# Attention masks added by TensorE inside the score banks, another opening, one routed expert moved, and later places in a decoder layer

## The reference

```python
k = _l2norm(silu(x @ Wk)); q = silu(x @ Wq); v = silu(x @ Wv); a = k * gamma
def step(S, inp):                         # scan over the tokens
    bs1 = einsum('bhk,bhkv->bhv', kt, S);  S1 = S + at[..., :, None] * bs1[..., None, :]
    S2 = exp(gft)[..., None] * S1
    bs2 = einsum('bhk,bhkv->bhv', kt, S2); S3 = S2 + at * bs2 + kt * vt
    o = einsum('bhk,bhkv->bhv', qt, S3)
out3 = stack([z, z, o]).reshape(B, 3*N, H, HD); out = out3[:, -N:]   # o of the tokens from 683 on
...
scores = q @ k^T / sqrt(HD); masked entries out; softmax; @ v; @ Wo + bo
...
top-2 of sigmoid(x @ centroids) + bias; gelu(x @ Wfc) @ Wproj of 2 shared and 2 chosen experts
```

## Time and profile before

| | |
|---|---|
| median of the runs | 2340.8 us |
| the profiled execution's own time | 2338.4 us |
| its span, first to last instruction | 2336.6 us |
| DVE busy | 2012.8 us (86%) |
| PE busy | 1754.3 us (75%) |
| POOL busy | 1189.1 us (51%) |
| ACT busy | 683.9 us (29%) |
| mean granted TensorE clock | 0.856 |

### The profile page before, as it was taken

How to read it: one execution, slowest core, us unless ns; L and a number is a source line. 1 busy time by engine, 2 the same in 40 slices (tenths; PEclk the granted TensorE clock), 3 DMA queues, 4 the chain that set the end, 5 groups by cost and what they waited for, 6 DMA issues and landing times.

```text
span 2336.6 us, 33767 instructions
## 1 busy us (share of the span) xinstructions
PE 1754.3 (75%) x10398; PEld 1333.6 (57%) x10398; DVE 2012.8 (86%) x5733; ACT 683.9 (29%) x1363; POOL 1189.1 (51%) x1487
## 2 busy tenths in 40 slices
PE   4258988998789879988998340268887699668993
PEld 2145766676667666766677220145575467555673
DVE  5999999999999999999999998999999989932000
ACT  1132234323432343234323110171223622143120
POOL 2544454565456545654675479473675655222203
PEclk8568999999999999998999765567998689977997
DMA  8100442344234423442345120000254024431353
GB/s 263 42 1 10 140 143 86 107 150 143 84 109 146 143 84 110 148 142 82 108 147 174 44 96 14 21 1 5 102 175 137 1 77 142 135 115 59 108 182 106
DMA packets 175118, 238.65 MB, mean 102 GB/s; under 512 B 28657, under 2 KB 148074, under 8 KB 174954
## 3 DMA queue, kind: packets, MB, share of 16 engines
q1 hardware_dynamic: 140874, 194.46, 24.6%
q10 hardware_dynamic: 27936, 25.44, 3.3%
q0 software_dynamic: 6144, 16.79, 2.2%
HBM read 202.09 MB, written 33.16 MB: 101 GB/s over the span
## 4 chain that ended last, share of the span: by engine, by line
DVE 52%; PE 22%; POOL 10%; issue 7%; ACT 6%; DMA 2%; SPq 0%; POOLq 0%; ACTq 0%; DVEq 0%; PEldq 0%
DVE ps L1610 11%; DVE ps L1591 10%; DVE prod L1583 7%; DVE terms L1598 7%; PE ps L646 4%; DVE terms L1593 4%; PE ps L637 4%; PE ps L582 2%; PE ps L573 2%; DVE rec_out L1537 2%; DVE rec_in L1537 2%; PE ps L519 2%; DVE oprod L1563 2%; ACT eT L847 1%; PE ps L530 1%
## 5 line engine op out<-in xcount | busy, mean ns | idle before, releaser
L1610 DVE TENSOR_REDUCE ps<-terms 128x64 f32<-128x320 f32 x1024 | 449.6, 485 | 0.0
L1591 DVE TENSOR_REDUCE ps<-prod 128x16 f32<-128x272 f32 x1024 | 398.3, 435 | 0.0
L1598 DVE TENSOR_TENSOR terms<-ps,rec_out 128x256 f32<-128x256 f32 x1024 | 382.8, 417 | 0.0
L1583 DVE TENSOR_TENSOR prod<-ps,rec_in 128x256 f32<-128x256 f32 x1024 | 381.9, 416 | 0.0
L637 PE MATMUL ps<-xg,fc 128*128 128x128 f32 x2848 | 351.6, 284 | 27.5 <-PE ps L646 11.9
L637 PEld LDWEIGHTS ps<-xg,fc 128*128 128x128 f32 x2848 | 341.4, 199 | 48.9 <-issue 41.2
L646 PE MATMUL ps<-pj,hT 128*128 128x256 f32 x1424 | 335.0, 389 | 33.2 <-ACT hT L926 33.2
L646 PEld LDWEIGHTS ps<-pj,hT 128*128 128x128 f32 x1424 | 266.3, 192 | 86.4 <-ACT hT L926 52.9
L573 PE MATMUL ps<-xtf,fc 128*128 128x512 f32 x512 | 244.1, 615 | 7.0 <-ACT hT L874 3.7
L582 PE MATMUL ps<-pj,hT 128*128 128x256 f32 x1024 | 238.9, 385 | 0.0
L582 PEld LDWEIGHTS ps<-pj,hT 128*128 128x128 f32 x1024 | 196.4, 193 | 57.5 <-issue 34.4
(11 more groups left out here) (235 smaller groups left out, 3061.0 us busy)
## 6 DMA issues: line engine op xcount, KB each, us to landing
fc<-in_wfcT SPq DMA_DIRECT2D x80, 1024.0 KB, 5.1
pj<-in_wpT SPq DMA_DIRECT2D x80, 1024.0 KB, 7.9
xg_rows<-in_rows ACTq DMA_DIRECT2D x105, 128.0 KB, 2.1
out_rows<-y ACTq DMA_DIRECT2D x89, 128.0 KB, 5.6
in_rows<-o_rows SPq DMA_DIRECT2D x2, 2176.0 KB, 17.4
out_rows<-o_rows SPq DMA_DIRECT2D x2, 2176.0 KB, 17.1
xtp<-in_xT SPq DMA_DIRECT2D x32, 128.0 KB, 2.6
xin<-in_x SPq DMA_DIRECT2D x8, 512.0 KB, 6.6
```

Of the source, the lines that this page charges most:

```text
L1583: tt(prod[:, c % PLACED, :, cols, 0:HD], SE[:, old, cols, 0:HD].unsqueeze(1).to_broadcast([P, NV, HC, HD]), rec_in[:, c].unsqueeze(2).to_b ...
L1591: red(SE[:, old, cols, HD:EH].rearrange("p v n -> p n v"), prod[:, c % PLACED, :, cols, 0:HD + 1], AX.X, ALU.add).then_inc(step_done, 1)
L1598: tt(terms[:, cols, :, 0:NV], SE[:, old, cols, HD:EH].unsqueeze(2).to_broadcast([P, HC, HD, NV]), rec_out[:, c].unsqueeze(1).to_broadcast( ...
L1610: red(SE[:, new, cols, 0:HD], terms[:, cols, :, 0:NV + 1], AX.X, ALU.add).then_inc(step_done, 1)
```

## The change

There are four parts.

1. **Masks.** For tiles 5 to 7 PE writes the mask into the score banks before the scores: for each group two products of the identity with `cap`, 308 columns each, and the query products are added to them. DVE's addition and its wait are gone.
2. **Opening.** The weights for keys and values are loaded second, those for queries later. PE makes keys, then values (`prepare_first`). ACT takes the keys' activation first, and a square root in place of POOL's power; DVE does the whole norm. The context's keys and values are made by ACT (`context`).
3. **Experts.** Tile 6 does experts 2 to 8 in its own period and leaves one, expert 9, which stands behind `start` in the tail; nothing stands behind `finish` there. SP's order follows it: `outputs(1)` of period 7 stands behind the reloads of experts 6 and 7.
4. **Places.** In the tables for bound tiles minima, divided, resid and routing stand later.

```diff
-REST = NE - 2
-BEHIND = {False: EXPERTS[LATE:], True: (REST, None, None, REST + 1, None)}
+FREE_REST = EXPERTS[LATE:]
+REST_OF = {FIRST_BOUND: (NE - 2, None, None, NE - 1, None), FIRST_BOUND + 1: (NE - 1, None, None, None, None), LAST: ()}
+def own_of(tile):
+    return EXPERTS[NSH:NE - len(rest_of(tile))]
...
             def period(p, m=None, f=None, load=None, bound=False, ahead=R, stores=(None,) * R):
...
-                    outputs(1)
-                    for e in EXPERTS[6:REST]:
+                    if f is None:
+                        outputs(1)
+                    for e in EXPERTS[6:8]:
                         used(m, e)
+                    if f is not None:
+                        outputs(1)
+                    if m != LAST:
+                        for e in own_of(m)[6:]:
+                            used(m, e)
...
-            for dst, src in ((w_f1, wf1), (w_g, wg), (w_kv, wkv), (w_q, wqr)):
+            for dst, src in ((w_kv, wkv), (w_f1, wf1), (w_g, wg)):
...
             def scores(m):

+                masked = m >= FIRST_BOUND
+                if masked:
+                    pe.wait_ge(cap_done, m + 1)
...
+                        if masked:
+                            for j in range(2):
+                                mm(ps[:, (UP, A0)[two] + j, 0:2 * QK * SK], ident[:, :], cap[:, b].unsqueeze(1).to_broadcast([P, 2 * QK, SK]),
+                                   start=True, stop=False)
...
-                                       start=True, stop=True, tile_position=(rows.start, 0))
+                                       start=not masked, stop=not masked or half == 1, tile_position=(rows.start, 0))
...
+            def prepare_first():
...
+                act.wait_ge(first_ps, 1)
+                fn(k, ps[:, KV[0], :].rearrange("p (i d) -> p i d", i=CH), ACT.Silu).then_inc(first_k, 1)
+                act.wait_ge(prep_pool, 3)
+                fn(hsum[:, 1], hsum[:, 0], ACT.Sqrt).then_inc(first_root, 1)
+                act.wait_ge(xf1_sb, 2 * CH)
+                fn(beta[:, :, :], graw[:, :, :], ACT.Sigmoid).then_inc(fq_sb, 1)
...
             def minima(t, m, at):
...
                         if m >= FIRST_BOUND:
-                            dve.wait_ge(cap_done, m + 1)
                             dve.wait_ge(sc_sb, m * (2 * B) + (2 * b + 2))
-                            tt(probs[:, b], probs[:, b], cap[:, b].unsqueeze(1).to_broadcast([P, H, SK]), ALU.add).then_inc(capped, 1)
-                        dve.wait_ge(capped, m * B + (b + 1))
+                        else:
+                            dve.wait_ge(capped, m * B + (b + 1))
                         red(least[:, b], probs[:, b], AX.X, ALU.min).then_inc(min_done, 1)
...
             def first_preparation():
...
+                dve.wait_ge(first_k, 1)
+                then(tt(zp[:, :], k, k, ALU.mult))
+                sums(hsum[:, 0])
...
+                then(nc.vector.tensor_scalar(hsum[:, 0], hsum[:, 0], NORM_EPS * NORM_EPS, None, ALU.max))
+                dve.wait_ge(first_root, 1)
+                then(nc.vector.reciprocal(hsum[:, 1], hsum[:, 1]))
...
-BOUND_AT = {"gated": 3, 0: 3, "x_plus": 12, 1: 13, "minima": (22, 22, 23, 24), "divided": 44, "resid": 53, 2: 53, "routing": 60, "places": 64, "rows": 65, "scatter": 66}
-LATER_AT = {"gated": 3, 0: 3, "x_plus": 13, 1: 13, "minima": (21, 22, 23, 24), "divided": 43, "resid": 49, 2: 49, "routing": 55, "places": 63, "rows": 63, "gather": 54, "scatter": 63, "combine": 66, 3: 75}
+BOUND_AT = {"gated": 3, 0: 3, "x_plus": 12, 1: 13, "minima": (22, 23, 24, 25), "divided": 48, "resid": 55, 2: 55, "routing": 62, "places": 64, "rows": 65, "scatter": 66}
+LATER_AT = {"gated": 3, 0: 3, "x_plus": 13, 1: 13, "minima": (22, 24, 25, 27), "divided": 46, "resid": 53, 2: 53, "routing": 60, "places": 63, "rows": 63, "gather": 54, "scatter": 63, "combine": 66, 3: 75}
```

More of the change, by code:

```diff
@@ L79, with rest_of @@
 LATE = NE - 5
-REST = NE - 2
-BEHIND = {False: EXPERTS[LATE:], True: (REST, None, None, REST + 1, None)}
+FREE_REST = EXPERTS[LATE:]
+REST_OF = {FIRST_BOUND: (NE - 2, None, None, NE - 1, None), FIRST_BOUND + 1: (NE - 1, None, None, None, None), LAST: ()}
+def rest_of(tile):
+    return [e for e in REST_OF.get(tile, FREE_REST) if e is not None]
+def own_of(tile):
+    return EXPERTS[NSH:NE - len(rest_of(tile))]
 STEP = 8
@@ L343, in period @@
                 if bound:
-                    used(f, REST)
+                    rest = rest_of(f) if f is not None else []
+                    for e in rest[:-1]:
+                        used(f, e)
                     if load is not None:
                         next_tile(load)
-                    used(f, REST + 1)
+                    for e in rest[-1:]:
+                        used(f, e)
                     outputs(0)
@@ L440, in prepare, with keys_or_values @@
                     mm(ps[:, low[i], D:2 * D], xf1T[:, i], w_f2, start=True, stop=True).then_inc(prep_b_ps, 1)
+            def prepare_first():
+                low = LOW[False]
+                xt = [[xtp[:, c].rearrange("p b (n i) -> p i b n", i=CH)[:, i] for c in range(KC)] for i in range(CH)]
+                def keys_or_values(half):
+                    for i in range(CH):
+                        for c in range(KC):
+                            ins = mm(ps[:, KV[half], i * D:(i + 1) * D], xt[i][c], w_kv[:, c, half * D:(half + 1) * D],
+                                     start=c == 0, stop=c == KC - 1)
+                    ins.then_inc(first_ps, 1)
+                pe.wait_ge(xt_in, 16 * KC)
+                for i in range(CH):
+                    for c in range(KC):
+                        mm(ps[0:HD, low[i], 0:P], w_f1[:, c], xt[i][c], start=c == 0, stop=c == KC - 1)
+                    for c in range(KC):
+                        ins = mm(ps[:, low[i], P:P + H], xt[i][c], w_g[:, c], start=c == 0, stop=c == KC - 1)
+                    ins.then_inc(prep_a_ps, 1)
+                keys_or_values(0)
+                for i in range(CH):
+                    pe.wait_ge(xf1_sb, i * 2 + 2)
+                    mm(ps[:, low[i], D:2 * D], xf1T[:, i], w_f2, start=True, stop=True).then_inc(prep_b_ps, 1)
+                keys_or_values(1)
             def turn(src, done):
@@ L718, in second @@
                         prep(2)
-                last_experts(f, (start, attend, weigh, finish, second), BEHIND[bound])
+                last_experts(f, (start, attend, weigh, finish, second), REST_OF.get(f, FREE_REST))
                 if m is not None:
@@ L736, in period @@
                 if m is not None:
-                    own = EXPERTS[NSH:NE if m == LAST else REST if bound else LATE]
+                    own = own_of(m)
                     bounds_of = bounds_of_tile[m]
@@ L984, in second @@
                         prep(2)
-                hi = last_experts(f, (start, attend, weigh, lambda: None, second), BEHIND[bound])
+                hi = last_experts(f, (start, attend, weigh, lambda: None, second), REST_OF.get(f, FREE_REST))
                 if bound and f is not None:
@@ L1009, in _ @@
             act.sem_inc(y_stored, 1)
-            prepare(0)
+            prepare_first()
+            context()
             act.wait_ge(pool_const, 1)
-            act.wait_ge(xattn_w_in, 10 * 16)
+            act.wait_ge(xattn_w_in, 11 * 16)
             for c in range(KC):
@@ L1246, in _ @@
             pool.wait_ge(pool_set, consts)
-            for i, op in enumerate(preparations(0)[:PREP_NORMS]):
-                prepare(0, i, op)
             def period(p, m=None, f=None, bound=False, keep=False):
@@ L1477, in first_preparation @@
                 k, w, e, z = vec[:, :, K_COL], vec[:, :, W_COL], vec[:, :, E_COL], vec[:, 0, W_COL:K_COL + 1]
-                done = PREP_NORMS
+                done = 0
                 def then(ins):
```

59 lines of the change are left out of this document (37 added, 22 removed).

## The result

The changed kernel takes 2332.5 us (median of 18 runs, 2322.1 to 2338.5), the kernel before beside it 2339.5 (18 runs, 2336.8 to 2344.2). The ratio is 0.9963, 95% interval 0.9951 to 0.9974: **7 us faster, where 27.5 were forecast**.

What follows compares the result with a forecast made beforehand. The chain was taken as opening, DVE's unbroken scan, then tail, with DVE holding 52% of the span. Gains of 13.8 (opening), 9.4 (scan) and 4.3 (tail) make 27.5: 2338.4 - 27.5 = 2310.9, plus 2.4: 2313 us, range 2304 to 2327.

Steps and rivals of the forecast that it cites:

- Opening: Start of the kernel: DVE reaches the first product with the decay at 19.7 instead of 33.54, 13.8 us earlier.
- what follows it is unchanged: Behind the start of the opening's layout: the transposes, then the scan, run as before.
- Router and experts: Tail: with no expert ahead, the router starts with the norm, -8.3 us; expert 8 hides in PE's idleness before the tail.
- The score stage: Tiles 5 to 7: a group takes 1.58 us with masks, 13.6 from first score product to last copy, 7.9 before.
- The 4 us a tile: Bound tiles' scores: by the skill's rule 32 bare weight loads of 0.13 us each, some 10 us higher over three tiles.
- Waits in the scan: DVE in periods 6 and 7: 4.6 of 14.0 us of removed additions turn into waits, leaving 9.4 us gained.
- The gate rows' clock: PE's gate rows behind the scores run at the upper clock: 4.5 us come back in period 6, 2.7 in period 7.
- waits eat the masks' gain: Rival in the scan: lower clock in one tile or bare identity loads, DVE gains nothing, 2322 us; chance 15%.
- Tail: Behind the scan: last score copy 5.7 us later, 1.67 of POOL wait gone, the chain then as before: +4.0 us.
- the lower clock: Rival in all three tiles' score stages: masks at PE's lower clock, 24.4 us a tile instead of 13.6, 2352 us; chance 4%.
- PE doesn't get done before the scan: Rival at the scan's end: expert 7 or 8 ends late, a pass of 8.8 us enters the chain, 2321 us; chance 7%.
- through 4 us before the scan: Scan's end: expert 7, behind which the store of the recurrence's outputs waits, ends 4 us before the scan.

Runs made afterwards that it cites:

- open_only: The kernel before with the new opening alone (prepare_first, context on ACT, new order of loads): 2326.0 us, ratio 0.9943 to before.
- f_none: The changed kernel with masks back on DVE and the old places, so opening and experts alone: 2322.6 us, ratio 0.9920 to before.
- experts_only: The kernel before with the experts' move alone, masks on DVE, opening and places as before: 2338.4 us, ratio 0.9981 to before.
- f_scan: The changed kernel with f32 masks on PE in tiles 5 and 6 only, DVE's additions in tile 7: 2323.5 us, ratio 0.9929 to before.
- tail_masks: The changed kernel with f32 masks on PE in tile 7 alone and the old places: 2334.7 us, ratio 0.9966 to before.
- store_first: The changed kernel with the recurrence's last store queued ahead of the load of expert 9's weights: 2329.7 us, ratio 0.9956 to before.
- rep: The changed kernel once more, unaltered, for a second profile: 2340.7 us, ratio 0.9988 to before.
- bf16_masks: The changed kernel with identity and mask of the mask products in bf16, scores still f32: 2325.2 us, ratio 0.9931 to before.
- masks_places: The kernel before with masks on PE and the new places, opening and experts as before: 2346.7 us, ratio 1.0026 to before.
- the square: Four kernels on one chip, all with opening and experts, f32 masks on PE in scan or not, tail or not: 2322.6, 2323.5, 2334.7, 2333.4 us.
- f_all: The changed kernel once more, f32 masks on PE in tiles 5 to 7: 2333.4 us, ratio 0.9966 to before.
- bf16_scan: The changed kernel with bf16 masks on PE in tiles 5 and 6, DVE's additions in tile 7: 2312.2 us, ratio 0.9883 to before.
- best: bf16_scan with the store of the recurrence's rows ahead of expert 9's weights: 2311.5 us, ratio 0.9874 to before.

## Why the prediction was wrong

**Opening: right.** Forecast 13.8 us, 13.94 in the profile at the layout's start, 13.4 by the ratio of `open_only`, which leaves 8.4 to 18.3 open. Its strings came out item by item: keys at 14.62 (14.6), ACT late with decay and beta (19.27; 19.4), DVE at the decay at 19.52 (19.7). That "what follows it is unchanged" is less sure. From there to the layout that opens period 6, where DVE has the same work, it is 1414 to 1417 us in the four profiles with the old opening (mean 1415.5) and 1415 to 1421 in the fourteen with the new one (mean 1417.8): some 2 us may be given back on the way, but the ranges overlap.

**Router and experts: right by the mechanism.** In the tail, from the residual sum behind the attention to the number of passes, it is 31.2 us before and 23.4 in `f_none`: 7.8, where 8.3 were forecast. Expert 8 is hidden, with 15.8 us of PE's idleness left in `f_none` and 9.05 in the changed kernel, 5 to 8 forecast. With no expert ahead PE stands 6.43 us and turns the rows at the lower level (1.94 instead of 1.06); that was in the forecast, whose 6.7 us to the shared experts came from such a turn and measure 6.65. What it lacked is this: in `experts_only` the stretch from that turn to the passes takes 20.6 us, in `f_none` 17.0, so only 4 of the 8 us are had. PE isn't the reason. Its rows up to the router's last product are the same in both (turn 1.94, router product 1.96, granted clock 0.67). But in `experts_only` ACT reads the router's result 1.9 us after it is made instead of at once, and four of DVE's small routing operations last 1.6 to 2.3 us, where each takes 0.19 in `f_none`. One of them, and what POOL does beside it:

```profile
2149.80 4.82 POOL L1091 TENSOR_TENSOR y_out<-y_out,y_back 128x1024 f32<-128x1024 f32 x2
2149.91 2.27 DVE L1411 TENSOR_TENSOR rbuf<-rbuf,index 128x32 f32<-128x32 f32 x1
```

In all profiles with the new order of experts such stretched operations lie inside POOL's two products of `y_back` and `y_out`, which combine tile 6's outputs. With the router's result read early, DVE starts 2.8 to 3.2 us ahead of the first of these and is through with the choice in time (the first profile of the changed kernel, `f_none`, `f_scan`, `tail_masks`, `store_first`); with it late by 2 us DVE starts 1.0 us ahead and loses the most (`experts_only`, `rep`, `bf16_masks`). So the earlier router has moved up against POOL's work; no run moves POOL's products to prove it, and why ACT reads late in some executions is open.

**The score stage: the step that failed.** The forecast took "A group's scores take 0.41" by halving a row of sixteen instructions, added 1.17 for the masks and got 1.58. The masks were nearly right (1.23). The 0.41 was never the time of one group: it is half of what two take side by side, and with a product of all 128 rows between them each takes its own 0.72. It makes 16.5 us of 13.6, in each of the three tiles. The page "TensorE: Matmul & The Clock Gate" of the Trainium skill, section "Part 3: Packing small matmuls — row/col tiling", says that a weight load overlaps a product in flight only if it goes to other row groups. Behind the mask products the rows agree: the small weights' loads begin with 0.42 us of idleness after the last mask load in f32 and 0.27 in bf16, together with the first small product. Against it stand, as the forecast said, the full-width turns, eight loads and eight product instructions in 1.06 us; but such turns have no two groups side by side to lose, so they couldn't price this. Nor is it shown that the bare loads cost anything here, as a group is 0.79 long with and without a mask product ahead of it. The 4 us a tile that I put beside the forecast by that rule were 2.9 by the stage, nearer than the forecast, by another way.

**Waits in the scan: right in kind, too small in size.** The rise in the scan's waits was put at 4.6 us; it is 8.0 in the profile and 11.0 in the second one. The 2.9 us of later scores are met again at the minima in period 6 (4.0, 1.4 forecast) and at "divided" in period 7 (6.4 and 9.3, 4.2 forecast), and `masks_places` shows how fixed the places are: 20 us between two tables for the same work. The gate rows' clock did come back: in period 6, from the turn of the gate's input to the end of the gate rows, the changed kernel takes 6.4 us instead of 10.7, so 4.3 returned of 4.5 forecast. The rival "waits eat the masks' gain" (15%, 2322) had the scan right, longer stage and no gain there; it missed the tail.

**Tail: the cover was counted, the length on the chain was not.** Forecast +4.0 for the masks; measured 12.1. Of this 8.7 is the stage, less 1.7 where the wait for POOL goes; that leaves 5, and in the profiles of the square what is left lies between the two table loads, where PE was at the lower level. The forecast let this stretch run "as before". A rival had the lower clock, but in the score products themselves, and these ran at the upper level in every profile.

**The store.** "PE doesn't get done before the scan" was a rival for 8.8 us, and a third of that came by another way: PE was done, but expert 7 ended so close to the scan that the fetch it frees went in ahead of the store, 3.1 us. The forecast counted expert 7 "through 4 us before the scan"; it was 2.1 (2023.67 against 2025.79, the end of the outputs' transposition). The forecast's own terms gave 1 to 3: 12.3 us of room before (2028.86 and 2041.15), less 7 to 9 for the scan, less 2 for PE.

So the terms without the masks, 22.1, came out at 19.1 (`f_none`), and the masks' gain of 5.4 (9.4 in the scan, scores later by 4.0 in the tail) turned into a cost of 10.8; what is left is the 8.3 us of `f_all`, all on one chip. That the masks are the part that failed is shown by taking them away and by the remedy: with their products a third as long and none of them in the tail, `bf16_scan` and `best` gain 27.4 and 29.5 us. That this is also the number of the forecast is chance: without masks in the tail the forecast's terms are 13.8 + 9.4 + 8.3 = 31.5. Open stays why the tail lost 5 us more than its longer stage explains.

## What to carry to other kernels

Price an instruction among the neighbours it will have, not among those of the row it is read from: two groups of small products in separate rows of the array cost 0.82 us together, and 0.72 each with a full-array product between them. A row that merges instructions of two groups doesn't say what one costs; look for a place where one stands alone. Work moved from a busy engine to an idle one is free only where the receiving engine isn't on the chain: the same masks came out even in the scan, where the longer scores came back as waits, and cost 12 us in the tail, so split such a change by stage, and take the narrowest type the values allow (here zeros and one large constant). And where a schedule has fixed places, one number that is 3 us off comes back at every later place.

## What the runs showed of the hardware

- A 128x308 product with f32 identity and mask takes 0.62 us at the upper clock (two of them, four recorded instructions, 1.23), with both in bf16 0.19 (0.38 for two). The page "FP8 and Floating Point Precision" of the Trainium skill, section "TensorE Precision Notes", gives true FP32 four passes; here the ratio of the two is 3.3.
- Executions of kernels with the same stage, from exponential to logarithm in the tail, differ there by 8 us: its turns of weights take 2.0 us each or 3.7 each by the level that was granted. The changed kernel spreads over 16 us in 18 runs, the kernel before over 7.
- Four f32 score products of 32 rows and 154 columns in one half of the array's rows are 0.79 us long, eight in both halves 0.82.
- DVE operations of 128x32 that take 0.19 us last 1.6 to 2.3 us in some executions of the router, four of them in `experts_only`. All of them lie beside POOL's two products of 128x1024 (3.74 and 4.82 us).
- A store that is queued 0.9 to 2.2 us behind the fetch of an expert's weights comes back 3 to 5.5 us later (9.1 to 11.7 instead of 6.2 us until DVE has the rows).
